# Written-out loops, and the experts' weighted answers added into the residual's rows by an accumulating indirect DMA

## The reference

```python
# layer 0: group norm, instance norm, 3x3 window attention over pixels, output projection
x = x + L0_conv(_gn(x), Wq, bq, Wk, bk, Wv, bv, Wo, bo)
# layer 1, on tokens t of shape [4, 4096, 256]
t = t + L1_attn(_ln_t(t), Wp, bp, Wg)       # gated running mean over the last 64 tokens
u = _ln_t(t)                                 # 16384 tokens of 256 channels
probs = softmax(u @ router_w.T)              # 8 experts
rw, re = top_k(probs, 2); rw = rw / rw.sum(-1)
out = u
for e in range(8):                           # float32 throughout
    y = gelu(u @ w1[e] + b1[e], exact) @ w2[e] + b2[e]
    out = out + combine[:, e] * y            # combine is rw where e was picked, else 0
t = t + out
x = tokens back to [4, 256, 64, 64]
```

## Time and profile before

| what | value |
|---|---|
| median of 3 runs | 2004.0 us |
| profiled execution, first to last instruction (span) | 1822.6 us |
| median less span (what lies around the instructions) | 181.4 us |
| loop 1, its 26 blocks in the hardware loop | 183.0 to 988.6 us |
| loop 2, first matmul of the first product to its last | 1129.9 to 1588.4 us |
| loop 3, first load issued to the end | 1611.4 to 1822.6 us |
| PE / DVE / ACT / POOL busy over the span | 76 / 67 / 52 / 47 % |

### The profile page before, as it was taken

One profiled execution on the slowest core, in us unless ns is written; L12 is line 12 of the kernel. 1 busy time (PEld: TensorE's weight loads), 2 busy tenths in 40 slices (PEclk: granted clock), 3 DMA queues, 4 the chain that ended last, 5 costly groups with the idle time before them and its releaser, 6 DMA issues. The chain is left out here.

```text
span 1822.6 us, 34262 instructions
## 1 busy us (share of the span) xinstructions
PE 1380.4 (76%) x8976; PEld 1218.9 (67%) x8977; DVE 1222.8 (67%) x4085; ACT 947.3 (52%) x2056; POOL 858.0 (47%) x872
## 2 busy tenths in 40 slices
PE   2398978888797879788879732999999999913333
PEld 2377867777776777677768631999999999912222
DVE  7467877877777778777878752666666666635554
ACT  0266655656464656455655413767777776601111
POOL 1324554645464646455554552566666666610000
PEclk9999998999898999898998855999999999955555
DMA  9507221212121212122221146455544554369997
GB/s 357 188 16 169 79 70 60 89 52 94 53 92 56 87 62 88 60 79 70 76 73 47 71 108 137 151 162 162 165 162 164 167 167 167 130 231 333 325 331 277
DMA packets 117759, 247.10 MB, mean 136 GB/s; under 512 B 40480, under 2 KB 54048, under 8 KB 113440
## 3 DMA queue, kind: packets, MB, share of 16 engines
q1 hardware_dynamic: 82848, 157.82, 28.5%
q0 software_dynamic: 26112, 71.60, 10.5%
q10 hardware_dynamic: 8704, 16.78, 2.4%
HBM read 132.57 MB, written 113.57 MB: 135 GB/s over the span
## 5 line engine op out<-in xcount | busy, mean ns | idle before, releaser
L1438 POOL DMA_INDIRECT answers<-yy,dest_i x288 | 303.6, 1054 | 178.8 <-DVE yy L1579 83.0
L1301 POOL DMA_INDIRECT sent<-tn,slot_s x256 | 249.8, 976 | 132.6 <-issue 71.9
L871 ACT ACTIVATE ex<-sm,shift 128x264 f32<-128x264 f32 x128 | 65.6, 512 | 290.6 <-DVE shift L1033 290.6
L1269 POOL TENSOR_TENSOR rs<-ve,halves 128x4 f32<-128x4 f32 x64 | 67.7, 1058 | 267.8 <-DVE ve L996 264.4
L1660 PE MATMUL m_bank<-ident,tot 128*128 128x128 f32 x256 | 63.0, 427 | 159.8 <-DVE tot L1645 159.8
L1528 ACT ACTIVATE hid<-m_bank,b1s 128x512 f32<-128x512 f32 x144 | 99.0, 687 | 134.7 <-issue 84.0
L1487 PE MATMUL s_bank<-w2h,hh 128*128 x576 | 166.0, 288 | 0.7 <-DVE yy L1579 0.7
L1660 PEld LDWEIGHTS m_bank<-ident,tot 128*128 128x128 f32 x256 | 50.2, 223 | 172.4 <-DVE tot L1645 172.4
L1487 PE MATMUL s_bank<-w2h,hl 128*128 x576 | 160.2, 278 | 0.0
L1487 PE MATMUL s_bank<-w2l,hh 128*128 x576 | 159.8, 277 | 0.0
L672 PE MATMUL m_bank<-wvo,band 128*128 128x258 f32 x960 | 140.0, 302 | 21.8 <-POOL band L1308 21.8
(11 more groups left out here) (224 smaller groups left out, 3964.2 us busy)
## 6 DMA issues: line engine op xcount, KB each, us to landing
xin<-sent SPq DMA_DIRECT2D x72, 516.0 KB, 3.8
got<-answers SPq DMA_DIRECT2D x32, 1024.0 KB, 7.4
xs<-in_x SPq DMA_DIRECT2D x32, 512.0 KB, 8.7
raw<-in_x SPq DMA_DIRECT2D x32, 512.0 KB
residual<-rsum SPq DMA_DIRECT2D x32, 512.0 KB, 2.9
res<-residual SPq DMA_DIRECT2D x32, 512.0 KB, 8.5
out_x<-fin ACTq DMA_DIRECT2D x32, 512.0 KB, 7.3
sent<-w_s SPq DMA_DIRECT2D x16, 512.0 KB, 8.8
```

What stands on the lines that cost most here:

```text
L1301: eng.indirect_dma_start(sent, bass.IndirectOffsetOnAxis(slot_s[:, par, j, k:k + 1], 0), tn[:, par, k, :], None).then_inc(scattered[par], 16)
L1438: eng.indirect_dma_start(answers, bass.IndirectOffsetOnAxis(dest_i[:, par, k:k + 1], 0), yy[:, par, k, :], None).then_inc(rows_out[par], 16)
```

## The change

1. `iterations` and `tiles_loop` no longer use `Fori`: every iteration of every loop is written out, with constant semaphore counts and addresses. The DVE's program grows from 877 to 3233 listed rows.
2. The rows sent to the experts grow from 258 to 260 floats and carry both weights; `mix` is gone, the weights are written into `tn`, and stage S waits for `Dmix` instead of `Dsl`.
3. `answers` is gone. `residual` becomes `summed`, one row for each token. In loop 2 the DVE picks the weight of each row, writes the answer to `yb`, multiplies it with the weight into `yy` (4 instructions more for a tile), and POOL's indirect DMAs add `yy` to the rows of `summed`. Since a token's two answers may come in neighbouring tiles, the DMAs of a tile wait until those of the tile before have landed.
4. Loop 3 only loads `summed` (512 KB a block, 4 buffers), transposes, copies (ACT one half of the channels, DVE the other) and stores.

```diff
         def iterations(eng, body):
-            for off in range(-2, 4):
-                body(Iteration(None, off, NB))
-            with eng.Fori(2, NB // 2 - 1) as half:
-                for off in range(2):
-                    body(Iteration(half, off, NB))
-            for off in range(NB - 2, NB + 3):
+            for off in range(-2, NB + 3):
                 body(Iteration(None, off, NB))
...
-                        done(route, eng.tensor_tensor(mix[:, bass.ds(prior.block("D") * KT, KT), :], p12[:, :, :],
+                        done(route, eng.tensor_tensor(tn[:, prior.parity("D"), :, C + 2:C + 4], p12[:, :, :],
                                                       psum2[:, :, :].broadcast_to([P, KT, 2]), ALU.mult))
...
                     if it.runs("S"):
                         par = it.parity("S")
-                        alone(eng, (route.sem, route.count(it.before(), "Dsl")))
+                        alone(eng, (route.sem, route.count(it.before(), "Dmix")))
...
                         alone(eng, (dest_ready.sem, dest_ready.count(it, "Yd")),
-                              *((y.sem, y.count(it, f"Yt{i}")) for i, y in enumerate(y_taken)))
+                              (yy_ready.sem, yy_ready.count(it, "Yy")))
+                        if it.block("Y") >= 1:
+                            eng.wait_ge(rows_out[1 - par], (it.block("Y") + 1) // 2 * 16 * KT)
                         for k in range(KT):
                             eng.indirect_dma_start(
-                                answers, bass.IndirectOffsetOnAxis(dest_i[:, par, k:k + 1], 0),
-                                yy[:, par, k, :], None).then_inc(rows_out[par], 16)
+                                summed, bass.IndirectOffsetOnAxis(dest_i[:, par, k:k + 1], 0),
+                                yy[:, par, k, :], None, compute_op=ALU.add).then_inc(rows_out[par], 16)
...
-                        eng.scalar_tensor_tensor(dest[:, par, :], xin[:, par, :, C + 1], column(expert_f, at_),
-                                                 xin[:, par, :, C], ALU.not_equal, ALU.add)\
-                           .then_inc(dest_ready.sem, 1)
+                        eng.tensor_copy(dest[:, par, :], xin[:, par, :, C]).then_inc(dest_ready.sem, 1)
+                        for j, op in ((0, ALU.is_equal), (1, ALU.not_equal)):
+                            last = eng.scalar_tensor_tensor(w_of[:, par, j, :], xin[:, par, :, C + 1],
+                                                            column(expert_f, at_), xin[:, par, :, C + 2 + j],
+                                                            op, ALU.mult)
+                        last.then_inc(pick_ready.sem, 1)
+                        pick_ready.wait(eng, it, "Xp")
+                        eng.tensor_tensor(weight[:, at_ % 4, :], w_of[:, par, 0, :], w_of[:, par, 1, :], ALU.add)\
+                           .then_inc(pick_ready.sem, 1)
...
+                        for k in range(KT):
+                            y_taken[k // 2].wait(eng, it, f"Yt{k // 2}")
+                            last = eng.tensor_scalar(yy[:, par, k, :], yb[:, k, :],
+                                                     weight[:, it.block("Y") % 4, k:k + 1], None, ALU.mult)
+                        last.then_inc(yy_ready.sem, 1)
...
+                for b in range(NB):
+                    if b >= DEEP:
+                        eng.wait_ge(turned[CC - 1], b - DEEP + 1)
+                    eng.dma_start(tot[:, b % DEEP, :, :].rearrange(flat), summed_v[b, :, :])\
+                       .then_inc(tot_in[b % DEEP], 16)
```

More of the change, by code:

```diff
@@ L1396, in tiles_loop @@
         def tiles_loop(eng, n, body):
-            for off in range(-2, 4):
-                body(Iteration(None, off, n))
-            with eng.Fori(2, n // 2 - 1) as half:
-                for off in range(2):
-                    body(Iteration(half, off, n))
-            for off in range(n - 2, n + 2):
+            for off in range(-2, n + 2):
                 body(Iteration(None, off, n))
@@ L1649, in _ @@
-                tiles_loop(eng, NB, body)
-            @block.tensor
-            def _(eng):
-                def body(it):
-                    if it.runs("K"):
-                        par = it.parity("K")
-                        tot_ready.wait(eng, it, "Kt")
-                        for c in range(CC):
-                            f_taken[c].wait_before(eng, it, f"Kk{c}")
-                            for k in range(KT):
-                                last = eng.transpose(m_bank[c][:, k * P:(k + 1) * P],
-                                                     tot[:, par, k, c * P:(c + 1) * P], ident[:, :])
-                            last.then_inc(f_full[c].sem, 1)
-                tiles_loop(eng, NB, body)
+                for _ in take_channels(eng, 1, eng.tensor_copy):
+                    pass
@@ L1665, in _ @@
             @block.scalar
             def _(eng):
-                def body(it):
-                    if it.runs("K"):
-                        par = it.parity("K")
-                        if it.base is not None or it.block("K") >= 2:
-                            eng.wait_ge(fin_out[par], it.pair("K") * 16)
-                        for c in range(CC):
-                            f_full[c].wait(eng, it, f"Kf{c}")
-                            eng.activation(fin[:, par, c, :], m_bank[c][:, :], ACT.Copy).then_inc(f_taken[c].sem, 1)
-                        blk = it.block("K")
-                        for i in range(CC):
-                            f_taken[i].wait(eng, it, f"Kk{i}")
-                        dst = ov[:, :, bass.ds(blk // IB, 1), bass.ds(blk % IB * BT, BT)]
-                        eng.dma_start(dst, fin[:, par, :, :]).then_inc(fin_out[par], 16)
@@ L1680, in _ @@
-                tiles_loop(eng, NB, body)
-                for i in range(2):
-                    eng.wait_ge(fin_out[i], 16 * (NB // 2))
+                for b in take_channels(eng, 0, lambda o, i: eng.activation(o, i, ACT.Copy)):
+                    for c in range(CC):
+                        eng.wait_ge(fin_taken[c], b + 1)
+                    eng.dma_start(ov[:, :, b // IB, b % IB * BT:(b % IB + 1) * BT], fin[:, b % DEEP, :, :])\
+                       .then_inc(fin_out[b % DEEP], 16)
@@ L1683, in hybrid @@
+                for i in range(DEEP):
+                    eng.wait_ge(fin_out[i], 16 * (NB // DEEP))
         loop3.close()
```

124 lines of the change are left out of this document (55 added, 69 removed).

## The result

The kernel after takes 2022.67 us (median of 4 runs, 2019.88 to 2024.72), the kernel before 2003.66 us beside it (2001.92 to 2004.92). The ratio is 1.010, with a 95% interval of 1.0081 to 1.012: the change costs 1 %, where 4.4 % less (1915 us, range 1870 to 1945) was forecast.

A forecast was written before the change was run, and what follows sets the result against it. It took PE to bound loop 2, DMA loop 3, and no full engine loop 1, held by jumps back and the `wx`/`band` collision; 2004 - 124 + 137 - 103 = 1914, stated as 1915 us, range 1870 to 1945.

The forecast's parts named there:

- The failed step: Loop 2, POOL: an accumulating DMA's issue costs what a plain write's does, 0.96 us, four taking 5.1 us a tile.
- issued or carried out at half the rate: Rival, loop 2, chance 0.25: accumulating issue 1.6 us, cycle 10.9 us, 2097 us in all; decides from a 9.6 us cycle.
- The landing: Loop 2: an accumulating DMA lands after a plain write's 1.45 us plus 1 us for the DRAM read.
- The chain: Loop 2: each tile's first DMA waits for the previous tile's landing, POOL's cycle 8.35 us against PE's 6.45, 137 us more.
- The time without accumulation: Loop 2: POOL's cycle at the price of a plain write, 0.8 + 5.1 + 1.45 = 7.35 us.
- Loop 2 against before: Loop 2 grows by 72 x (8.35 - 6.45) = 137 us, bounds 65 and 443 us.
- Loop 1, jumps back: Loop 1: writing the loop out removes DVE idle time at jumps back, 2.6 us a block, 67 us over 26 blocks.
- Loop 1, late scatter: Loop 1: later scatters move `band` back and free `wx`; blocks of 26.2 us, 124 us gained together with writing out.
- Loop 3: Loop 3: traffic falls from 2 MB to 1 MB a block at 329 GB/s, 103 us less, bounds 80 to 115.
- The 181 us: Whole kernel: the median lies 181.4 us above the profiled span of 1822.6 us, kept constant in the sum.
- a DVE that binds: Rival, loop 2, chance 0.05: DVE multiplications and POOL's issue hinder each other, up to 3 us a tile, about 2050 us.

The follow-up runs named there:

- the plain write: The kernel after with a plain indirect write where it accumulates in loop 2, waits unchanged: 1816.16 us, ratio 0.908 to before.

## Why the prediction was wrong

- **The failed step** is "The issue I leave as it is, because the instruction still names 128 rows". An accumulating issue takes 1.56 us and not 0.96, and one of the four up to 2.04: 2.44 us a tile, 176 us over 72 tiles. This was the rival "issued or carried out at half the rate", which named an issue of 1.6 us, a cycle of 10.9 us and a turning point of 9.6. The cycle came to 10.1 us. That POOL builds twice the reads, the rival's condition, no run shows; what the traces show is 53760 packets in the queue against 26112, with the same bytes. The sign follows from this term alone: without its 176 us the kernel after would stand at 2023 - 176 = 1847 us, 8 % under before, and in the quick condition at 1870 - 176 = 1694 us, 7 % under. With the plain write, which takes the added landing away too, it is 9 % faster than before where it was timed.
- **The landing** was right: I counted 1 us more for the read, and the gap to the next tile is 0.8 us longer in the median (2.52 us, 1.72 with the plain write); how much of it is the read no run shows. The chain (next tile's first DMA behind the landing) was right too. But the sum put the DVE's 0.8 us from `yy` to the first DMA into it, and `yy` is ready 4.5 us early: the gap is 2.5 us, not 0.8 + 1.45 + 1 = 3.25. The time without accumulation came to 6.88 us in the median, 7.24 in the mean, for 7.35.
- **Loop 2 against before.** The 6.45 us a tile were those of the quick condition. Where the change was timed, before needed 7.5, so the loss was 194 us and not the 264 of the quick condition. This hid a part of the wrong price.
- **Loop 1, jumps back:** 67 us forecast; 71 us from putting the loop back, 58 us from writing out alone, 42 us in the quick condition. The step is right. For the condition of the profile its size was too large: the DVE's two idle times at the jumps back are 30.0 and 17.1 us over the whole first profile, 47 in all, and the 67 came from taking one block (block 3) as the measure of all 26.
- **Loop 1, late scatter:** that a later `band` frees `wx`, the border between 0.55 and 0.77 us and the blocks of 26.2 us were right in the condition of the profile (57 us forecast, 58 measured; blocks of 26.9 us; 91 us gained in all of the 124, the wider rows and the rest included). In the first profile the 26 blocked `wx` start 0.37 to 0.64 us ahead of `band` and the free ones 0.77 us or more. So the order of the starts alone doesn't decide: the blocked ones start first and wait all the same. Where the change was timed the late scatter was worth nothing, because `wx` wasn't blocked there before either, and loop 1 gave 49 us.
- **Loop 3:** 103 us less forecast, 127 measured. The term was mis-sized, and 127 is outside its bounds of 80 to 115: I took before's 329 GB/s, after ran at 413 GB/s. Part of the 127 lies in the turn from loop 2, which both measures contain.
- **The 181 us** that I kept constant were a difference between two conditions, not time around the span. I had written that no row excluded that this time depends on the program; the right reading was that the rows and the median did not belong together.
- **Small slips** that change nothing: the DVE's share of a tile in the earlier trace rows is 4.18 us, not 4.15, and a DVE that binds at 6.9 + 3 = 9.9 us a cycle would give 2025 us, not 2050.

The terms that were measured add up to the result: -49 + 194 - 127 = +18 us, against +19 between the medians. Set against the forecast's -124 + 137 - 103 = -90, the miss of 108 us is 75 in loop 1, 57 in loop 2 and 24 the other way in loop 3. In the condition of the profile the miss would be 137 us: 33 in loop 1, 127 in loop 2 (10.1 instead of 8.35 us a tile, the price of the issue) and 23 the other way in loop 3. So the condition took 42 us from the gain of loop 1 and 70 us from the loss of loop 2; the number alone would have hidden both.

What stays open: why PE's results are released late in one condition while POOL issues indirect DMAs, and what sets the condition. It is shown that in loop 1 they move with the scatters, and that neither the hardware loops nor the longer rows of `sent` bring them. POOL's issues alone don't bring them either: loop 2 of after has none. Why the adding form's issue is longer, and why its rows go in packets of their own, is open too. No kernel here that leaves nothing out beats all others in both conditions. The late scatter with written-out loops and the loops 2 and 3 of before beats before and after in both (0.942 to 0.945, 0.968).

## What to carry to other kernels

Price an accumulating DMA by the time that its issue takes of its engine (here 0.6 us more for each, 2.44 a tile), not by its landing alone (0.8 us a tile); when nothing in the trace shows it, work out the sign of the whole at the upper bound too before counting on the nearest row. Traffic saved in one loop is worth little if it is paid in a chain that stands for every tile of another (here 127 us gained in loop 3, 194 lost in loop 2). When a span and the median differ by a tenth, the profile may be of another condition than the times, as here: take a second profile before counting anything from the first. And when a row names an engine as what ended a wait, count whose instruction it is: two that one landing releases look like cause and effect.

## What the runs showed of the hardware

- An indirect DMA that adds: 1.56 us of POOL for 128 rows of 1 KB (kernel after), against 0.96 for a write (the plain write); landing 0.8 us later (median); one packet of 1024 bytes for each row, where the write puts four rows into 4096 bytes.
- One kernel at 1824 us and at 2003 us, without a change in it. In the slow condition semaphore updates of PE come up to 6.05 us behind the product (6.26 us in the kernel after with loop 1 in a hardware loop), and one wait on such an update is 7.4 us long; in the nine profiles of the quick one none that ended a wait comes more than 0.035 us behind. In loop 2 of the kernel after, the updates that `hid` waits for come at most 0.015 us behind their products (141 of them), though POOL issues there for 7.6 of 10.1 us.
- `wx`, with two SBUF inputs, is held up by `band` when it starts 0.37 to 0.64 us ahead of it, and free from 0.77 us on (first profile of before, 26 blocked and 57 free).
- `band` ahead of the scatters is 5 % worse than the late scatter in one condition (1798.55 against 1717.97) and 3 % better in the other (1875.42 against 1938.93).
